# Attention block in exact-split fp32 on one core: Strassen's seven block products for the first product and the scores

## What is computed

```python
h = group_norm(hidden_states, norm_gamma, norm_beta)
q = conv1x1(h, wq, bq)
k = conv1x1(h, wk, bk)
v = conv1x1(h, wv, bv)
attn = jnp.einsum('bci,bcj->bij', qf, kf) * scale
attn = jax.nn.softmax(attn, axis=2)
out = jnp.einsum('bcj,bij->bci', vf, attn).reshape(B, C, H, W)
out = conv1x1(out, wo, bo)
return residual + out
```

## Time and profile before

| | us |
|---|---|
| median of 3 runs | 2144.74 |
| lowest, highest | 2144.32, 2145.11 |
| span of the profiled execution, from its first to its last instruction | 2145.2 |
| PE busy in it | 2121.6 (99%) |
| PE weight loads | 1753.5 (82%) |
| DVE busy | 1381.5 (64%) |
| ACT busy | 673.7 (31%) |
| POOL busy | 192.5 (9%) |

### The profile page before, as it was taken

One profiled execution on the slowest core, in us unless ns is written; L12 is line 12 of the kernel. 1 busy time (PEld: TensorE's weight loads), 2 busy tenths in 40 slices (PEclk: granted clock), 3 DMA queues, 4 the chain that ended last, 5 costly groups with the idle time before them and its releaser, 6 DMA issues.

```text
span 2145.2 us, 25470 instructions
## 1 busy us (share of the span) xinstructions
PE 2121.6 (99%) x9328; PEld 1753.5 (82%) x9328; DVE 1381.5 (64%) x2219; ACT 673.7 (31%) x1113; POOL 192.5 (9%) x92
## 2 busy tenths in 40 slices
PE   6999999999999999999999999999999999999999
PEld 5878888888888888888888888888888888888887
DVE  6466584756757567575675847658475685756746
ACT  3241322413334132332413224132241333324232
POOL 1010100101000010010100101010000100001000
PEclk9999999999999999999999999999999999999999
DMA  3102001020110202001020010200102020010101
GB/s 123 40 1 79 1 31 50 1 79 1 41 39 1 79 1 80 1 12 67 1 80 1 20 59 0 80 1 36 44 1 79 1 79 1 9 71 1 40 0 40
DMA packets 31520, 73.33 MB, mean 34 GB/s; under 512 B 4640, under 2 KB 4640, under 8 KB 31392
## 3 DMA queue, kind: packets, MB, share of 16 engines
q1 hardware_dynamic: 29136, 71.31, 9.1%
q10 hardware_dynamic: 2256, 0.27, 0.1%
HBM read 38.02 MB, written 33.55 MB: 33 GB/s over the span
## 4 chain that ended last, share of the span: by engine, by line
PE 97%; issue 1%; POOL 1%; DMA 0%; DVE 0%; SPq 0%; ACT 0%; POOLq 0%; DVEq 0%
PE bank L243 32%; PE bank L244 32%; PE bank L245 32%; DMA xt<-in_wv 0%; POOL p_lo L207 0%; POOL all_max L212 0%; POOL rstd L217 0%; POOL all_max L227 0%; SPq L174 0%; SPq L173 0%; DVE stage L686 0%; DVE stage L680 0%; DVE run_max L651 0%; DVE h_lo L558 0%; DVE t_lo L642 0%
## 5 line engine op out<-in xcount | busy, mean ns | idle before, releaser
L243 PE MATMUL bank<-t_hi,h_hi 128*128 128x512 f32 x1024 | 399.3, 390 | 3.0 <-DVE t_lo L642 2.9
L245 PE MATMUL bank<-t_hi,h_lo 128*128 128x512 f32 x1024 | 398.8, 390 | 0.0
L244 PE MATMUL bank<-t_lo,h_hi 128*128 128x512 f32 x1024 | 398.8, 389 | 0.0
L243 PE MATMUL bank<-p_hi,v_hi 128*128 128x512 f32 x1024 | 398.3, 389 | 0.0
L244 PE MATMUL bank<-p_lo,v_hi 128*128 128x512 f32 x1024 | 398.3, 389 | 0.0
L245 PE MATMUL bank<-p_hi,v_lo 128*128 128x512 f32 x1024 | 398.3, 389 | 0.0
L444 ACT COPY scores<-bank 128x512 f32<-128x512 f32 x256 | 145.9, 589 | 397.7 <-PE bank L245 397.3
L448 ACT ACTIVATE scores<-scores 128x512 f32<-128x512 f32 x256 | 159.8, 628 | 325.1 <-DVE scores L656 325.0
L243 PEld LDWEIGHTS bank<-t_hi,h_hi 128*128 128x128 f32 x1024 | 192.6, 188 | 43.9 <-issue 3.3
L651 DVE TENSOR_TENSOR run_max<-run_max,scores 128x512 f32<-128x512 f32 x192 | 132.9, 692 | 146.9 <-ACT scores L444 142.9
L244 PEld LDWEIGHTS bank<-t_lo,h_hi 128*128 128x128 f32 x1024 | 192.7, 188 | 39.9
(11 more groups left out here) (83 smaller groups left out, 2715.1 us busy)
## 6 DMA issues: line engine op xcount, KB each, us to landing
out<-stage SPq DMA_DIRECT2D x128, 256.0 KB, 2.1
xt<-in_x SPq DMA_DIRECT2D x15, 2048.0 KB, 8.1
xt<-in_x SPq DMA_DIRECT2D x4, 512.0 KB, 12.1
scores<-in_wk SPq DMA_DIRECT2D x4, 256.0 KB, 5.0
scores<-in_wq SPq DMA_DIRECT2D x4, 256.0 KB, 5.2
xt<-in_wo SPq DMA_DIRECT2D x1, 1024.0 KB, 8.1
xt<-in_wv SPq DMA_DIRECT2D x1, 1024.0 KB, 10.6
stage<-in_bv ACTq DMA_DIRECT2D x1, 256.0 KB, 13.1
```

The source lines that it names most:

```text
L243: nc.tensor.matmul(o, a_hi, b_hi, start=start, stop=False)
L244: nc.tensor.matmul(o, a_hi, b_lo, start=False, stop=False)
L245: return nc.tensor.matmul(o, a_lo, b_hi, start=False, stop=stop)
```

## The change

**Blocks.** wkq is cut into 2 x 2 blocks of 256 x 256, and h into 2 x 2 blocks of 256 x 512. Strassen's method (in Winograd's form) makes a 2 x 2 block product of seven block products of sums instead of eight. T is made so: seven products (`t_product`) of sums of wkq's blocks (made and split once in setup, `wt_hi`, `wt_lo`) with A11, A12, A22 and the sums S1 to S4 of h's blocks (`sum_h`, `low_h`, once an image). The scores are made so too, from the same seven blocks of h and seven sums of T's blocks. T: 2 row blocks x 7 products x 2 k x 3 = 84 matmuls; scores: 28 products x 2 x 3 = 168. V keeps its 96 (with A11, A12, S1, A22 and three weight blocks), the output sums their 192.

**Sums.** What the seven products add to each other is partly accumulated in PSUM; in between ACT copies a bank's partial sum to SBUF (`snap` in T, three a row block; `snap_s` in the scores, three for each q), and DVE adds such snapshots to other banks (`add_t`, six a row block; `add_s`, three for each q). All of T is made before the scores, and all scores, of both halves, before V; the softmax's maximum is taken of both halves together, in seven steps of 1024 columns, and V is what PE does next. `centre` and `exponentials` work on two blocks (1024 columns) at a time; `add_up` is three instructions of 2048, 1024 and 512 columns.

**SBUF.** The split weights of T (2 x 3584 columns) and of V (2 x 3072) share `w_split`; they are kept in DRAM (`kept_t`, `kept_v`) and reloaded for each image. T's parts, V's and P's share `big_hi` and `big_lo`. The whole x of the next image no longer fits while the scores are made: it is loaded by eight pieces of 256 KB for its statistics, again whole after the scores, and x of the present image once more, by halves, for the residual (`rest`). The loop holds one image and runs 15 times.

The core of the diff:

```diff
+T_ORDER = (4, 5, 2, 7, 6, 1, 3)
+S_ORDER = tuple((7, q) for q in range(4)) + tuple(
+    (p, q) for pair in ((0, 1), (2, 3)) for p in (1, 6, 5, 3, 2, 4) for q in pair)
...
         def images(engine, image):
-
-
-            with engine.Fori(0, B - 2, 2) as b:
-                image(b, 0, True)
-                image(b + 1, 1, True)
-            image(B - 2, 0, True)
-            image(B - 1, 1, False)
+            with engine.Fori(0, B - 1) as b:
+                image(b, True)
+            image(B - 1, False)
...
+            def image(b, more):
+                sp.wait_ge(t_summed, count(b, 14, 14))
+                sp.dma_start(w_split[:, :, 0:VW].bitcast(F32), kept_v).then_inc(wvs_in, 16)
...
+                            sp.wait_ge(bn_set, count(b, PIECES, PIECES + n - 1))
...
+                    sp.wait_ge(v_summed, count(b, 8, 8))
+                    sp.dma_start(w_split[:].bitcast(F32), kept_t).then_inc(wt_in, 16)
...
+            def image(b, more):
+                if more:
+                    deviation(b + 1)
+                for half in range(2):
+                    pool.wait_ge(max_step, count(b, MAX_STEPS, MAX_STEPS))
+                    pool.sem_inc(reduce_begun, 1)
+                    nc.gpsimd.partition_all_reduce(wide[:, half, :], red[:, half, :], P, MAX_ALL).then_inc(max_all, 1)
...
+            def t_product(b, r, p):
+                at = {4: alpha_t, 2: alpha_t, 6: alpha_t, 3: alpha_t, 7: beta_t, 5: eps_t, 1: eps_t}[p][r]
+                for k in range(2):
+                    mm = product(bank[at][:], wt_hi[:, p - 1, k, cols(r)], wt_lo[:, p - 1, k, cols(r)],
+                                 h_hi[:, OF_H[p], k, :], h_lo[:, OF_H[p], k, :],
+                                 k == 0 and p in (4, 7, 5), k == 1 and p in (3, 7, 1))
+                mm.then_inc(t_summed, 1)
...
+                        if p == 6:
+                            pe.wait_ge(t_snapped, count(b, 6, 3 * r + 2))
...
+            def image(b, more):
+                make_t(b)
+                make_scores(b)
+                make_v(b)
+                pe.wait_ge(v_split, count(b, 8, NJ))
+                outputs_0(b)
+                outputs_1(b)
+                if more:
+                    pe.wait_ge(wt_in, count(b, 16, 16))
...
+            def image(b, more):
+                for r in range(2):
+                    if r == 0:
+
+                        act.wait_ge(h_split, count(b, 7, 7))
+                        snap(b, 0, 0, "a", T_AT[4])
+                    high_t(b, r, "D3")
+                    snap(b, r, 1, "b", T_AT[2])
+                    snap(b, r, 2, "y", T_AT[6])
...
+                low_v(b, 0)
+                low_v(b, 1)
+                for g in range(4):
+                    centre(b, 0, g)
+                for g in range(4):
+                    low_v(b, 2 + g)
+                    low_p(b, 0, 2 * g)
+                    low_p(b, 0, 2 * g + 1)
+                for g in range(4):
+                    centre(b, 1, g)
+                low_v(b, 6)
+                add_up(b, 0)
+                low_v(b, 7)
```

More of the change, by code:

```diff
@@ L46, in attention_program @@
     HALF = N // 2
+    QUARTER = C // 2
     CG = C // GROUPS
@@ new lines, in attention_program, with low, high @@
+        first_v_hi, first_v_lo = (a[:, NJ:NJ + 6, :].rearrange("p (b k) n -> p b k n", k=2) for a in (big_hi, big_lo))
+        def low(a):
+            return a[:, :, 0:QUARTER]
+        def high(a):
+            return a[:, :, QUARTER:C]
+        b11, b12, b21, b22 = low(wkq[:, 0:2, :]), high(wkq[:, 0:2, :]), low(wkq[:, 2:4, :]), high(wkq[:, 2:4, :])
+        d1, d2, d3, neg_d4 = (wd_t[:, n, :].rearrange("p (k n) -> p k n", k=2) for n in range(4))
+        wt_from = {1: b11, 2: b21, 3: b22, 4: neg_d4, 5: d1, 6: d2, 7: d3}
@@ new lines, in high_wt @@
+            def high_wt(p):
+                if p in (4, 5, 6, 7):
+                    act.wait_ge(wd_set, {5: 1, 6: 2, 7: 3, 4: 4}[p])
+                else:
+                    act.wait_ge(wkq_copied, KC)
+                nc.scalar.activation(wt_hi[:, p - 1, :, :], wt_from[p], ACT.Identity,
+                                     scale=-1.0 if p == 2 else 1.0).then_inc(wt_high, 1)
+            act.wait_ge(wov_copied, KC)
+            act.wait_ge(bias_summed, 1)
+            for n in range(2):
+                nc.scalar.copy(first_v_hi[:, n, :, :], wov[:, 2 * n:2 * n + 2, :]).then_inc(wvs_high, 1)
@@ new lines, in _ @@
+            act.wait_ge(wdv_set, 1)
+            nc.scalar.copy(first_v_hi[:, 2, :, :], wide[:, 0:2, :]).then_inc(wvs_high, 1)
+            act.wait_ge(wq_split, KC)
+            for k in range(KC):
+                act.wait_ge(wkq_summed, k + 1)
+                nc.scalar.copy(wkq[:, k, :], bank[KC + k][:]).then_inc(wkq_copied, 1)
+            for k in range(KC):
+                normalise(0, k)
+            high_h(0, 0)
+            for p in T_ORDER:
+                high_wt(p)
+            for n in range(1, 7):
+                high_h(0, n)
@@ L655, in centre, with maximum @@
+            halves = scores[:].rearrange("p (s j) n -> p s j n", s=2)
+            def maximum(b, step, j):
+                if step:
+                    dve.wait_ge(max_step, count(b, MAX_STEPS, step))
+                before = halves[:, :, 0, :] if step == 0 else red[:]
+                nc.vector.tensor_tensor(red[:], before, halves[:, :, j, :], ALU.max).then_inc(max_step, 1)
+            def centre(b, half, g):
                 dve.wait_ge(max_all, count(b, 2, half + 1))
-                nc.vector.tensor_tensor(scores[:, j, :], scores[:, j, :], all_max[:], ALU.subtract).then_inc(centred, 1)
+                j = half * NJ + 2 * g
+                nc.vector.tensor_tensor(scores[:, j:j + 2, :], scores[:, j:j + 2, :],
+                                        wide[:, half, :].unsqueeze(1).to_broadcast([P, 2, HALF]),
+                                        ALU.subtract).then_inc(centred, 1)
@@ new lines, in add_up @@
+            def add_up(b, half):
+                e = scores[:, half * NJ:(half + 1) * NJ, :]
+                at = count(b, SUM_STEPS, 3 * half)
+                nc.vector.tensor_tensor(e[:, 0:4, :], e[:, 0:4, :], e[:, 4:8, :], ALU.add).then_inc(sum_step, 1)
+                dve.wait_ge(sum_step, at + 1)
+                nc.vector.tensor_tensor(e[:, 0:2, :], e[:, 0:2, :], e[:, 2:4, :], ALU.add).then_inc(sum_step, 1)
+                dve.wait_ge(sum_step, at + 2)
+                nc.vector.tensor_tensor(red[:, half, :], e[:, 0, :], e[:, 1, :], ALU.add).then_inc(sum_step, 1)
```

924 lines of the change are left out of this document (543 added, 381 removed).

## The result

The changed kernel takes **2450.19 us** (median of 4 runs, 2445.41 to 2451.09), the kernel before beside it 2144.93 us (4 runs, 2144.32 to 2145.86): a ratio of 1.142, 95% interval 1.1404 to 1.1436, so 14.2% slower. The forecast was 2410 us, the range 2290 to 2475. The span of the profiled execution is 2448.6 us. The first lines are the page of the profile: busy times, the granted clock in 40 slices, the chain that ended last, and the groups with the most idle time before them, which answer to the earlier trace rows. PE's busy time counts overlapping records (0.39 us long and 0.23 us apart from 1375.55 us on), so its share says less than the idle times do.

A forecast was written before the change was run, and what follows sets the result against it. The prediction took TensorE's matmuls as the bound of the kernel before, with PE waiting for nothing. For the change, setup 69 + 16 images x 146.4 - 6.2 (last image) + 4.3 (tail) = 2410 us, range 2290 to 2475.

The forecast's parts named there:

- The forecast's largest wait: Before the output sums: PE waits for all eight low parts of V, with only V as cover for the softmax; 13.0 us.
- The two reloads: Weight loads for V (after T) and T (after V): 12 and 15 us, beside scores and outputs, costed at nothing.
- wait in V: In V, block 6 needs a low part that DVE makes behind the centrings; 1.6 us with semaphore and copy.
- waits in T: In T, PE waits for ACT's second snapshots, as DVE is 6.0 us late: 2.6 and 2.3 us, together 4.9.
- POOL's 6.1 us: On POOL, a reduction behind the power instruction of `deviation` starts 6.1 us after its input is ready.
- the rival that let VectorE keep up: DVE's chain from V's start to its last low part fits under V: 2110 us in total; chance 5%.
- the 1.7 us at the loop's end: DVE idle at the loop's end, once an image, counted into its 6.0 us lateness at T.
- C22: In the scores: needed 19 us after T's end, while the next image's pieces land some 13 us after it; no cost.
- The two terms of the forecast: PE's clock loss per image: 3.0 us after the 13 us wait before the outputs, 1.5 us for one in T.
- the rival that the clock stays up: PE comes back at 1.00 after its waits, so 4.5 us an image aren't lost: 2338 us; chance 8%.
- the heavier rival: A slower total than forecast, 2475 to 2540 us, partly from slow matmuls in V behind short waits; chance 13%.
- start T in effect at 69 us: Setup: T starts in effect at 69 us, 27 us later than before, bounds 62 to 82.

The follow-up runs named there:

- the swap: Changed kernel with ACT taking T's second snapshot ahead of D3's high part, in both row blocks: 2375.63 us, ratio 1.107 to the kernel before.
- full load later: Changed kernel with the full load of the next x issued behind the two max reductions: 2426.93 us, ratio 1.1314 to the kernel before.
- the output experiment: Changed kernel with PE waiting for each low part of V before that block's output sums, not all eight before the first: 2330.93 us, ratio 1.0866.
- the tail: Changed kernel with four order edits, plus half 0's reciprocal later, half 1's sum earlier, and `rest` reloads one block behind their stores: 2187.49 us.
- the last kernel: Changed kernel with four order edits and three later moves, plus half 1's residual loaded into free slots of `room`: 2106.42 us, ratio 0.9813.

## Why the prediction was right, and where it was off

**The mechanism.** PE fell from bound to waiting, behind DVE's list between the last maximum and V's last low part. The forecast's largest wait (before the first output sum, released by V's low part, sixteen times) is there, and the experiment that lets PE start without that low part takes 119 us away. The matmuls, 8848 in 16 images, left as counted. The two reloads are hidden, as said.

**The sum.** The terms add up to 2409.5 us, and the span is 39.1 us above that. The first output matmul stands at 182.61 us, where my terms give 69 + 19.0 + 4.9 + 1.5 + 38.1 + 21.8 + 1.6 + 13.0 = 168.9: 13.7 us. Fourteen images at 148.3 for 146.4: 26.8 us. The last one, 139.2 for 140.2, and the end, 50.4 for 50.8, give 1.4 us back. That the total came within 1.6% is in part luck: the waits before the outputs and in T were put 3.6 us an image too high, those in V and the scores 3.4 us too low.

**An image, term by term.**

| | forecast | measured |
|---|---|---|
| wait before the output sums | 13.0 | 11.0 |
| wait in V | 1.6 | 3.9 |
| waits in T | 4.9 | 3.3 |
| waits in the scores | 0 | 1.1 |
| clock | 4.5 | 5.2, by subtraction |
| restarts of the five waits | 0 | 1.4 |
| matmuls | 122.4 | 122.4 |
| image | 146.4 | 148.3 |

- *Outputs and V.* Together 14.9 for 14.6: the sum held and the split did not. The step that was mis-sized is POOL's 6.1 us: it is 7.4 to 9.0 here, as a load of 2 MB runs then that the earlier trace rows did not have beside it: in the trace of before no DMA engine is busy from 1304 to 1310 us (share 0.00). The first centrings (5.50 us for four, 4.5 in the forecast) were slower as well, the second four were not (4.62); it is the first of the four alone, 2.09 us for 1.21. V's block 6 came later by both; what V lost the outputs did not lose again.
- *Wide DVE instructions.* Records of 1024 elements last 1.2 us and of 2048 2.28, and they come 1.14 us apart, and 2.31 before one that waits for them, where 1.13 and 2.19 + 0.12 were taken. Right; the rival that let VectorE keep up is out.
- *T.* The mechanism (a snapshot on ACT behind D3) is shown by the swap. In the image above the waits are 1.25 and 2.25 us for 2.6 and 2.3. The step that was too large is the 1.7 us at the loop's end: DVE goes from the last of the outputs into T with no idle time:

```profile
1419.85 0.69 DVE L919 TENSOR_TENSOR scores<-scores 128x512 f32<-128x512 f32 x1
1420.46 0.75 DVE L807 SCALAR_TENSOR_TENSOR scores<-bank,t_step,scores 128x512 f32<-128x512 f32 x1
```

- *Scores.* Costed at nothing, wrongly. I looked at C22 alone, a block of the scores' product, needed 19 us after T's end. The wait is later, before a product whose bank ACT's snapshot must free, and ACT waits there for DVE, which has done the pieces late. The step named the queue (the pieces behind V's weights); moving them ahead of it removed all of the 1.1 us.
- *Clock.* The two terms of the forecast, 3.0 and 1.5 us, are what the earlier trace rows give: behind 8.97 us idle 14 matmuls took 6.1 us at a granted clock of 0.50, where 14 x 0.2267 = 3.2 would do, and behind 2.90 us idle seven took 3.1 us for 1.6. Two places were priced: 3.0 us behind the outputs' wait (some 2.4 by subtraction) and 1.5 in T, where it is 1.8 in eight images and nothing in seven, 1.0 in the mean. There the rival that the clock stays up held in part. A third place, behind the V wait, which the sum put at nothing, runs at 0.57 and costs some 1.8. Slow matmuls in V behind short waits were one of the two reasons for the heavier rival (2475 to 2540 us); they came, and the total stayed below it. The restarts, 1.4 us an image, stood in no term. The clock is 5.2 of 148.3 us, 3.5%, and it returns with the waits in every image.
- *Setup.* Taken to start T in effect at 69 us. PE's timeline there, then two windows of it:

```profile
36.82 3.63 PE L325 MATMUL bank<-bq_s,scores 128*128 128x1 f32 x32
40.30 0.49 PE L329 MATMUL bank<-vecs,big_hi 128*128 128x1 f32 x2
...
53.88 0.77 PE L294 MATMUL bank<-big_hi 128*128 128x512 f32 x1
...
67.27 0.79 PE L294 MATMUL bank<-h_hi,w_split 128*128 128x512 f32 x1 [8.73 <-DVE w_split L772]
76.70 0.79 PE L294 MATMUL bank<-h_hi,w_split 128*128 128x512 f32 x1 [6.50 <-DVE h_lo L721]
82.99 0.79 PE L294 MATMUL bank<-h_hi,w_split 128*128 128x512 f32 x1 [3.37 <-ACT scores L553]
```

```profile
36.00:40.00 4.00, 4.00 (x35) 3.84 (x33) 0.00 (x0) 0.00 (x0) 0.00 (x0) 1.00 0.00 0
40.00:54.00 14.00, 14.00 (x69) 14.00 (x69) 0.00 (x0) 0.00 (x0) 0.00 (x0) 0.51 0.00 0
```

  The 48 one-column matmuls, from 36.82 to 53.88 us, take 17.1 us and not 12 (inside the bounds of 6 and 21). T's second product starts at 76.7 us for 67.7: 9.0 us, of which 0.8 are there when they begin, 5.1 are the one-column matmuls, and 3.1 lie in ACT's and DVE's lists behind them, which begin at 54.1 us. Eight of the twelve matmuls that follow run at the lower clock (0.50) too, but no idle time of ACT or DVE there is put down to them. A third wait, 3.4 us for a snapshot, follows. Of the 13.7 us, 10.1 stand at T's end (104.45 us for 94.4), 1.4 are the scores', and 2.3 V and the wait behind it.

**Left open.** Why the clock fell behind T's second wait in eight images and not in seven, and in all fifteen with the full load later, isn't shown. The 28 us by which the output experiment fell short are named (low parts of P, T) but not divided. The three moves of the tail were not tried one by one. That DVE's first centring is slow because POOL reduces the second half at the same time (1344.54 to 1346.42 us, beside the centring that starts at 1344.66) is only argued: no run took that reduction away, and in the last image, with the same reduction beside it, that centring lasts 1.69 us and not 2.09.

## What to carry to other kernels

Cutting matmuls from a kernel whose TensorE never waits saves time only as far as the other engines' chain between two products stays under the matmuls that cover it: before you count the saving, add up that chain from the last input it needs to the first product that needs it, and look for the one wait that asks for all blocks at once. Here the saving of 8.2 us an image was turned into a loss of 17.6 by an order of work, not by the amount of it: small moves in the order and a place for one half's input took 344 us off, the whole loss of 305 and 39 more. Price an instruction order on POOL, ACT and a DMA queue as carefully as that of TensorE, and expect each wait that you take away to show the next one.

## What was not expected of the hardware

- The gap between a power instruction and a reduction on POOL, 5.95 to 6.38 us alone, is 7.4 to 9.0 us when a load of 2 MB runs through it; one changed line showed it.
- Each wait of PE costs 0.24 to 0.31 us beyond its idle time, at a granted clock of 1.00 before and behind it. Five waits are some 1.4 us of an image.
- The granted clock does not go by the wait alone. Behind 2.04 to 2.46 us idle before V (full load later, 15 images, 2.28 us in the window below) it stayed at 1.00, and in the same kernel it fell behind the 2.24 us in T in all 15. In the changed kernel it fell behind 2.25 us in T in eight images of 15, and behind 3.5 to 5.1 us before V in all. Behind the 0.24 to 0.78 us waits of the last kernel's later images it stayed. The full load later:

```profile
1335.00:1340.00 5.00, 4.15 (x18) 3.44 (x19) 4.09 (x8) 4.94 (x9) 0.00 (x0) 1.00 0.65 266
```

- The 48 one-column fp32 matmuls leave two records each (32 for the first 16, 64 for the other 32). The first 16 come 0.22 us apart (36.82 to 40.30) at a granted clock of 1.00, the other 32 come 0.42 us apart (40.30 to 53.88) at 0.51: the clock fell with no idle time of PE before it, while all that it did was these.
